# Adding a carried state to the first element of each scan on ScalarE, with VectorE's scans starting from zero

## The chip, the core and the metric

The kernel runs on one core of one Trainium2 chip. The metric is the device time of one execution, in microseconds (us). The core's engines run side by side and meet through semaphores: TensorE (PE; its weight loads are PEld), VectorE (DVE), ScalarE (ACT), GpSimd (POOL) and SyncE (SP), which here issues the DMAs.

## The reference, cut to what matters

The whole reference is a two-layer model: patches and a Fourier embedding, a gated recurrent attention, a mixture of experts, a Mamba block, and a feed-forward part on the upper half of the tokens. Only the Mamba block's recurrence is touched:

```
A = -jnp.exp(A_log)
def step(h, t):
    dt_t, B_t, C_t, u_t = t
    h = h * jnp.exp(dt_t[:, :, None] * A) + (dt_t * u_t)[:, :, None] * B_t[:, None, :]
    y = jnp.einsum('bds,bs->bd', h, C_t)
    return (h, y)
```

There are 4 sequences, 128 inner channels and 32 states for each, so 4096 independent recurrences for each sequence. The value that a recurrence carries is `h`; the factor `exp(dt * A)` is called the decay and the addend `dt * u * B` the input.

## The kernel before, in words

Time is cut into three thirds of G = 368 tokens (index k = 0, 1, 2). One third of one sequence is a segment; the 12 segments run in the order of all four sequences of the first third, then the second, then the third. A segment has NSTEP = 16 steps, one after the other, 192 in all, numbered t. A step handles two halves h = 0 and 1, each 128 recurrences (4 channels by 32 states, on the 128 partitions) over 368 tokens. The recurrence over the tokens of one half is one VectorE instruction, a scan (L1618), `state = decay * state + input`, with an initial state.

What a step t takes, engine by engine:

- PE `spread_input(t)` (L721, two matmuls) spreads the rows of dt*u over the partitions into PSUM banks 2 and 3, and `spread_step(t)` (L731, two matmuls) the rows of dt into banks 4 and 5 or 6 and 7, by the parity of t. `spread_step(t)` waits until both scans of step t-2 are done, because they read the same banks. After it, in even steps, `add_y` (L749, eight matmuls for two steps) sums up the outputs of steps t-4 and t-3; this stands ahead of the next step's matmuls in PE's queue.
- ACT `decay(t)`: two Exp instructions in place in PSUM (all of ACT's calls go through a helper and show as L896), one for each half. Then `carry_on(t-1)` copies the last column of step t-1's two halves into `scan_carry`, for the same rows of the same sequence 64 steps later.
- DVE `input_term(t)` (L1602) multiplies both halves of the spread input by B into the ring buffer `bx`, and `scan_half(t, h)` (L1618) does a scan into `hbuf`.
- POOL `output_term(t)` (L1258) multiplies both halves of `hbuf` by C.

Every fourth step (t % 4 == 3, `shared(t)`) the product with B is POOL's (L1266) and not VectorE's. For that, ACT copies the spread input out of PSUM with `move_input(t+4)`, one cycle of four steps ahead; this copy stands in ACT's queue directly ahead of `decay(t)` of a shared step, and on PE `spread_input(t+4)` stands directly ahead of `spread_step(t)`. The order on VectorE in a cycle around a shared step s is thus: scan(s-2, 1), scan(s-1, 0), scan(s-1, 1), scan(s, 0), input(s+1), scan(s, 1), scan(s+1, 0), input(s+2), scan(s+1, 1), scan(s+2, 0), input(s+3), and so on: four scans in a row around each shared step. The order on each engine is that of the code; nothing rearranges it. Once in a segment VectorE also multiplies the finished outputs by the gate (L1624), and POOL splits the next segment's rows (L1279, L1285).

In the first third (64 steps) a scan starts from the constant 0.0; in the other two (128 steps, 256 scans) its initial state is a column of `scan_carry`.

Of the kernel before, what the change touches and what calls it, by code (L numbers as in the profile page):

```python
# [10 lines left out]
ALU = mybir.AluOpType  # L11
ACT = mybir.ActivationFunctionType
# [3 lines left out]
B, C, T, V = 4, 64, 128, 64  # L16
# [18 lines left out]
DI, DS, DTR, KC = 128, 32, 16, 4  # L35
NSEG = B * NG
NRING = 4
DB = 32
NQ = DB // (128 // DS)
NSTEP = DI // (128 // DS) // 2  # L40
# [36 lines left out]
def build(nc, x, txt, wdft, wts, wexp, bn, out, dbg=None):  # L77
    lay, nw = places(WEIGHTS)
    elay, ne = places(EXPERTS)
    with ExitStack() as ctx:  # L80
# [5 lines left out]
        def s(name):  # L86

            if name not in sems:
                sems[name] = ctx.enter_context(nc.semaphore(name))
            return sems[name]  # L90

        PS = ctx.enter_context(nc.psum_tensor("PS", [128, 8, 512], F32))
# [105 lines left out]
        def shared(t):  # L198
            return t % 4 == 3
# [4 lines left out]
        def own_to(t):  # L204
            return t + 1 - (t + 1) // 4
# [21 lines left out]
        hbuf, hcbuf, bx = ring(0), ring(1), ring(2)  # L227
        carry = sb("scan_carry", [128, B * DS])
# [663 lines left out]
        def _(act):  # L892
# [223 lines left out]
            def decay(t):  # L1116

                seg, i = t // NSTEP, t % NSTEP
                act.wait_ge(s("dt_spread"), t + 1)
                for h in range(2):  # L1120
                    g = (2 * (i % 2) + h) * NQ + i // 2
                    bank = 4 + 2 * (t % 2) + h
                    f(PS[:, bank, 0:G], PS[:, bank, 0:G], ACT.Exp, scale=aneg[:, g:g + 1]).then_inc(s("decay"), 1)

            act.wait_ge(s("a_ready"), 1)
            def move_input(t):

                act.wait_ge(s("x_spread"), inputs_to(t))
                if t >= 4:
                    act.wait_ge(s("bx_ready"), t // 4)  # L1130
                f(moved, PS[:, 2:4, 0:G], ACT.Copy).then_inc(s("x_moved"), 1)

            def carry_on(t):
# [2 lines left out]
                act.wait_ge(s("scanned"), 2 * (t + 1))  # L1136
                f(carry[:, b * DS + 2 * i:b * DS + 2 * i + 2], hbuf[t % NRING][:, :, G - 1], ACT.Copy).then_inc(s("carried"), 1)

            move_input(3)
            for t in range(NSEG * NSTEP):  # L1140
                if shared(t) and t + 4 < NSEG * NSTEP:
                    move_input(t + 4)
                decay(t)
                if 1 <= t <= CARRIED:
                    carry_on(t - 1)
            for g in range(NGR + 2):
                if g < NGR:
                    p, k = groups[g]
                    act.wait_ge(s("mo_ps"), g + 1)
                    f(P1[:, p, cols(k)], PS[:, g % 2, 0:G], ACT.Copy).then_inc(s("mo_ev"), 1)  # L1150
                if g >= 2:
                    p, k = groups[g - 2]
# [25 lines left out]
            for b in range(B):  # L1178
                for y in range(2 * NG):
# [3 lines left out]
                      bias=col("b1a" if y < NG else "b1b")).then_inc(s("hid_ready"), 1)  # L1183
# [125 lines left out]
        def _(dve):  # L1309
# [204 lines left out]
            for n in range(NG * E + 1):  # L1514
# [7 lines left out]
                if n and n % E == 0:  # L1522
                    k = n // E - 1
# [80 lines left out]
            def scan_half(t, h):  # L1604

                seg, i = t // NSTEP, t % NSTEP
                b, k = seg % B, seg // B
                if h == 0:
                    if shared(t):
                        dve.wait_ge(s("bx_ready"), t // 4 + 1)  # L1610
                    else:
                        dve.wait_ge(s("b_used"), own_to(t))
                    if t >= NRING:
                        dve.wait_ge(s("hc_ready"), t - NRING + 1)
                        dve.wait_ge(s("carried"), min(t - NRING + 1, CARRIED))
                dve.wait_ge(s("decay"), 2 * t + h + 1)
                a = b * DS + 2 * i + h
                nc.vector.tensor_tensor_scan(hbuf[t % NRING][:, h, :], PS[:, 4 + 2 * (t % 2) + h, 0:G], bx[t % NRING][:, h, :],  # L1618
                                             carry[:, a:a + 1] if k else 0.0, ALU.mult, ALU.add).then_inc(s("scanned"), 1)

            def finish_y(seg):

# [16 lines left out]
            for g in range(NGR + 2):  # L1639
                if 1 <= g <= NGR:  # L1640
                    p, k = groups[g - 1]
# [6 lines left out]
                if g >= 2:  # L1648
                    p, k = groups[g - 2]
# [154 lines left out]
```

## Time and profile before

| | us |
|---|---|
| median of 3 runs | 1072.88 (1071.45 to 1074.3) |
| the profiled execution's own time | 1069.42 |
| its span, first to last instruction | 1067.3 |
| PE / DVE / ACT / POOL busy | 835.7 / 800.2 / 512.5 / 542.3 |
| the 64 steps with initial state 0.0 | about 489 to 641 of the span |
| the 128 steps with a carried state | about 641 to 955 of the span |

Busy time is an average over stages with different limits; the change acts only in the last line's stage. A row of the timeline gives the start of a group of like instructions, how long the group lasts, and their count; where a bracket stands, the engine had been idle for so long and the named one released it. DVE instructions overlap a little: the next starts before the one ahead has ended.

### The profile page before, as it was taken

Reading aid. Unit: us, or ns where it says so; the run is one execution under the profiler, and the core shown is the slowest. Engines: PE = TensorE matmul, PEld = TensorE weight load, DVE = VectorE, ACT = ScalarE, POOL = GpSimd, SP = SyncE. Lnnn points to the kernel's source line nnn. Section 1 sums busy time; section 2 is a strip of 40 time slices with the busy share of each in tenths; the row PEclk is TensorE's granted clock in tenths of the full one; section 3 lists DMA queues with packets and bytes.
Section 4 is the critical chain, followed back from the end, with each engine's and each line's share of the span. In section 5 each row is a group of like instructions: output and inputs, shape, how many; then the busy total and the mean of one; then the engine's idle time right before and its main releaser. Section 6 shows DMA issues by size and latency. Waiting matters only on the chain.

```text
span 1067.3 us, 11533 instructions
## 1 busy us (share of the span) xinstructions
PE 835.7 (78%) x3813; PEld 356.5 (33%) x3813; DVE 800.2 (75%) x1054; ACT 512.5 (48%) x1015; POOL 542.3 (51%) x356
## 2 busy tenths in 40 slices
PE   7873665767865997976887878878888878879887
PEld 4441334646733333431121111111111111115465
DVE  1248998865532444389999999999999999984475
ACT  1365300185252775664555555555554444434621
POOL 0010749420010000016999999999999999880100
PEclk9987855687565999995667685665556576659987
DMA  9100000700100000011011011011011011000001
GB/s 389 41 0 1 0 0 20 154 1 1 60 1 0 2 2 0 1 29 35 22 43 27 17 43 38 8 40 40 9 38 43 10 34 43 1 0 1 1 16 28
DMA packets 20505, 33.09 MB, mean 31 GB/s; under 512 B 10078, under 2 KB 19294, under 8 KB 19422
## 3 DMA queue, kind: packets, MB, share of 16 engines
q1 hardware_dynamic: 20446, 32.36, 10.7%
q8 instruction: 30, 0.49, 0.2%
q14 instruction: 29, 0.24, 0.1%
HBM read 17.57 MB, written 1.20 MB: 18 GB/s over the span
## 4 chain that ended last, share of the span: by engine, by line
PE 40%; DVE 32%; issue 12%; ACT 9%; POOL 4%; SPq 1%; DMA 1%; DVEq 0%; ACTq 0%; POOLq 0%
DVE pair_arrays L1618 14%; DVE pair_arrays L1602 5%; PE PS L574 4%; PE PS L749 4%; PE PS L721 3%; PE PS L420 3%; PE PS L731 3%; PE PS L510 2%; PE PS L841 2%; ACT PS L896 2%; ACT token_weights L896 2%; PE PS L481 2%; DVE pair_arrays L1424 2%; PE PS L867 2%; ACT pair_arrays L896 2%
## 5 line engine op out<-in xcount | busy, mean ns | idle before, releaser
L1258 POOL TENSOR_TENSOR pair_arrays<-pair_arrays 128x736 f32<-128x736 f32 x192 | 332.4, 1743 | 25.7 <-DVE pair_arrays L1618 25.1
L896 ACT ACTIVATE PS<-PS,A_negative 128x368 f32<-128x368 f32 x384 | 191.3, 538 | 130.1 <-PE PS L731 129.5
L1618 DVE TENSOR_TENSOR_SCAN pair_arrays<-PS,scan_carry,pair_arrays 128x368 f32<-128x368 f32 x256 | 237.1, 972 | 0.4
L1602 DVE TENSOR_TENSOR pair_arrays<-pair_arrays,PS 128x736 f32<-128x736 f32 x144 | 129.7, 901 | 8.4 <-PE PS L721 8.3
L749 PE MATMUL PS<-pair_arrays,weights 128*32 128x368 f32 x768 | 134.1, 730 | 1.2 <-POOL pair_arrays L1258 1.1
L1212 POOL TENSOR_TENSOR big<-pair_arrays 128x1104 f32<-128x1104 f32 (+15 forms) x32 | 55.9, 1766 | 131.1 <-DVE pair_arrays L1375 68.5
L1618 DVE TENSOR_TENSOR_SCAN pair_arrays<-PS,pair_arrays 128x368 f32<-128x368 f32 x128 | 110.6, 909 | 2.7 <-ACT PS L896 2.7
L721 PE MATMUL PS<-spread_rows,token_weights 96*128 96x368 bf16 x192 | 68.5, 452 | 37.8 <-DVE pair_arrays L1602 24.1
L1266 POOL TENSOR_TENSOR pair_arrays<-pair_arrays,token_weights 128x736 f32<-128x736 f32 x48 | 83.9, 1747 | 18.4 <-DVE big L1580 18.4
L721 PE MATMUL PS<-pair_arrays,token_weights 96*128 96x368 bf16 x192 | 67.2, 445 | 25.9 <-DVE pair_arrays L1602 20.1
L481 PE MATMUL PS<-big,weights 128*128 128x368 f32 (+15 forms) x192 | 62.7, 493 | 31.3 <-DVE big L1435 20.1
L1279 POOL TENSOR_TENSOR pair_arrays<-big 128x368 f32<-128x368 f32 x24 | 18.8, 803 | 123.2 <-PE PS L651 123.2
L731 PE MATMUL PS<-pair_arrays,token_weights 96*128 96x368 bf16 x192 | 68.3, 451 | 13.9 <-DVE pair_arrays L1618 12.5
L731 PE MATMUL PS<-spread_rows,token_weights 96*128 96x368 bf16 x192 | 69.9, 460 | 11.0 <-DVE pair_arrays L1618 9.4
L896 ACT ACTIVATE pair_arrays<-pair_arrays 128x69 f32<-128x69 f32 (+4 forms) x46 | 27.7, 607 | 96.3 <-DVE pair_arrays L1424 74.5
L896 ACT ACTIVATE pair_arrays<-PS,weights 128x368 f32<-128x368 f32 (+1 forms) x66 | 38.4, 594 | 53.2 <-PE PS L841 33.0
L481 PEld LDWEIGHTS PS<-big,weights 128*128 128x128 f32 x192 | 45.2, 286 | 49.1 <-issue 30.3
L896 ACT ACTIVATE scan_carry<-pair_arrays 128x2 f32<-128x2 f32 x128 | 26.3, 206 | 69.9 <-DVE pair_arrays L1618 69.5
L896 ACT ACTIVATE token_weights<-PS 128x736 f32<-128x736 f32 (+2 forms) x66 | 44.2, 671 | 29.3 <-PE PS L721 23.9
L574 PE MATMUL PS<-pair_arrays,big 64*64 64x368 f32 x576 | 53.6, 496 | 4.3 <-issue 1.7
L896 ACT ACTIVATE pair_arrays<-PS,bn_shift,bn_scale 128x736 f32<-128x736 f32 x48 | 43.9, 960 | 24.9 <-PE PS L574 24.9
L896 ACT ACTIVATE pair_arrays<-PS 64x256 f32<-64x256 f32 (+5 forms) x48 | 19.8, 426 | 69.4 <-PE PS L510 18.2
(190 smaller groups left out, 1244.1 us busy)
## 6 DMA issues: line engine op xcount, KB each, us to landing
big<-in_x SPq DMA_DIRECT2D x4, 2048.0 KB, 17.3
big<-decay_rows SPq DMA_DIRECT2D x4, 1104.0 KB, 16.3
spread_rows<-pair_arrays SPq DMA_DIRECT2D x96, 46.0 KB, 1.9
pair_arrays<-pair_arrays SPq DMA_DIRECT2D x96, 46.0 KB, 1.9
spread_rows<-big SPq DMA_DIRECT2D x48, 46.0 KB, 1.9
pair_arrays<-big SPq DMA_DIRECT2D x48, 46.0 KB, 1.9
weights<-in_wts SPq DMA_DIRECT2D x1, 2204.0 KB, 18.0
big<-in_wexp SPq DMA_DIRECT2D x1, 1536.0 KB, 7.8
```

Source lines behind the costliest of these rows:

```text
L420: last = nc.tensor.matmul(PS[:, TOK_BANKS[b][i], 0:nm * V], Wtok[:, q].rearrange("p h o -> p (h o)"), xs[:, b, m0:m0 + nm, q, :], start=(q ...
L481: last = nc.tensor.matmul(PS[:, NG * p + k, 0:size], w("ones"), prod[n % 4][:, k * size:(k + 1) * size], start=True, stop=True)
L574: last = nc.tensor.matmul(PS[half((b2 + p) % 2), bank + p, 0:G], weight[half(b2), 64 * b2:64 * b2 + 64], data[half(b2), p, :], start=start ...
L721: last = nc.tensor.matmul(PS[:, 2 + h, 0:G], pick[:, (i // 2) * 128:(i // 2 + 1) * 128], high(stack[seg % 2][1][0:3 * DB, 2 * (i % 2) + h] ...
L731: last = nc.tensor.matmul(PS[:, 4 + 2 * (t % 2) + h, 0:G], pick[:, (i // 2) * 128:(i // 2 + 1) * 128], high(stack[seg % 2][0][0:3 * DB, 2 ...
L749: last = nc.tensor.matmul(PS[r:r + DB, seg % 2, 0:G], w("ysel")[:, (i // 2) * DB:(i // 2 + 1) * DB], hcbuf[t % NRING][:, h, :], start=Fals ...
L896: return nc.scalar.activation(o, i, fn, **kw)
L1212: nc.gpsimd.tensor_tensor(prod[n % 4][:, 0:NC * (L - lag)].rearrange("p (c r) -> p c r", r=L - lag), chunks(q_[:, p, :])[:, :, lag:L], chu ...
L1258: nc.gpsimd.tensor_tensor(hcbuf[t % NRING], hbuf[t % NRING], c4(seg).unsqueeze(1).to_broadcast([128, 2, G]), ALU.mult).then_inc(s("hc_read ...
L1266: nc.gpsimd.tensor_tensor(bx[t % NRING], b4(t // NSTEP).unsqueeze(1).to_broadcast([128, 2, G]), moved, ALU.mult).then_inc(s("bx_ready"), 1)
L1602: tt(bx[t % NRING], b4(seg).unsqueeze(1).to_broadcast([128, 2, G]), PS[:, 2:4, 0:G], ALU.mult).then_inc(s("b_used"), 1)
L1618: nc.vector.tensor_tensor_scan(hbuf[t % NRING][:, h, :], PS[:, 4 + 2 * (t % 2) + h, 0:G], bx[t % NRING][:, h, :], carry[:, a:a + 1] if k e ...
```

## The change

For steps of the second and third third, ScalarE gets two more instructions after `decay(t)`: `bx[:, h, 0] = decay[:, h, 0] * carry + bx[:, h, 0]`, each on one column, with the carry as the scale and the old first input as the bias, both columns in memory with one value for each partition. The scans then all take the constant 0.0 as their initial state, and those with k > 0 wait for the new instruction too.

```diff
+            def carry_in(t):
+
+                b, i = t // NSTEP % B, t % NSTEP
+                act.wait_ge(s("carried"), t - B * NSTEP + 1)
+                act.wait_ge(s("decay"), 2 * t + 2)
+                if shared(t):
+                    act.wait_ge(s("bx_ready"), t // 4 + 1)
+                else:
+                    act.wait_ge(s("b_used"), own_to(t))
+                for h in range(2):
+                    first = bx[t % NRING][:, h, 0:1]
+                    f(first, PS[:, 4 + 2 * (t % 2) + h, 0:1], ACT.Identity, bias=first,
+                      scale=carry[:, b * DS + 2 * i + h:b * DS + 2 * i + h + 1]).then_inc(s("carry_in"), 1)
...
                 decay(t)
+                if t >= B * NSTEP:
+                    carry_in(t)
                 if 1 <= t <= CARRIED:
                     carry_on(t - 1)
...
+                if k:
+                    dve.wait_ge(s("carry_in"), 2 * (t - B * NSTEP) + h + 1)
                 dve.wait_ge(s("decay"), 2 * t + h + 1)
-                a = b * DS + 2 * i + h
                 nc.vector.tensor_tensor_scan(hbuf[t % NRING][:, h, :], PS[:, 4 + 2 * (t % 2) + h, 0:G], bx[t % NRING][:, h, :],
-                                             carry[:, a:a + 1] if k else 0.0, ALU.mult, ALU.add).then_inc(s("scanned"), 1)
+                                             0.0, ALU.mult, ALU.add).then_inc(s("scanned"), 1)
```

ScalarE's queue around a shared step of a carried segment, before: the step ahead, the copy `move_input` (token_weights is the name of its target's memory), the two decays, `carry_on`.

```order
L896 ACTIVATE PS<-PS,A_negative 128x368 [waits dt_spread]
L896 ACTIVATE PS<-PS,A_negative 128x368
L896 ACTIVATE scan_carry<-pair_arrays 128x2 [waits scanned]
L896 ACTIVATE token_weights<-PS 128x736 [waits bx_ready,x_spread]
L896 ACTIVATE PS<-PS,A_negative 128x368 [waits dt_spread]
L896 ACTIVATE PS<-PS,A_negative 128x368
L896 ACTIVATE scan_carry<-pair_arrays 128x2 [waits scanned]
```

The same place of the changed kernel (the memory of `bx` goes by the name pair_arrays):

```order
L896 ACTIVATE PS<-PS,A_negative 128x368 [waits dt_spread]
L896 ACTIVATE PS<-PS,A_negative 128x368
L896 ACTIVATE pair_arrays<-PS,pair_arrays,scan_carry 128x1 [waits b_used,decay,carried]
L896 ACTIVATE pair_arrays<-PS,pair_arrays,scan_carry 128x1
L896 ACTIVATE scan_carry<-pair_arrays 128x2 [waits scanned]
L896 ACTIVATE token_weights<-PS 128x736 [waits bx_ready,x_spread]
L896 ACTIVATE PS<-PS,A_negative 128x368 [waits dt_spread]
L896 ACTIVATE PS<-PS,A_negative 128x368
L896 ACTIVATE pair_arrays<-PS,pair_arrays,scan_carry 128x1 [waits bx_ready,decay,carried]
L896 ACTIVATE pair_arrays<-PS,pair_arrays,scan_carry 128x1
L896 ACTIVATE scan_carry<-pair_arrays 128x2 [waits scanned]
```

The two new instructions stand between the decays and `carry_on` in each of the 128 steps, and the first waits for both decays; no table load was added. On VectorE nothing changes its place. There, before, the two scans of a shared step with the next input between them:

```order
L1618 SCALAR_TENSOR_TENSOR pair_arrays<-PS,scan_carry,pair_arrays 128x368 [waits carried,decay,hc_ready,bx_ready]
L1602 TENSOR_TENSOR pair_arrays<-pair_arrays,PS 128x736 [waits x_spread]
L1618 SCALAR_TENSOR_TENSOR pair_arrays<-PS,scan_carry,pair_arrays 128x368 [waits decay]
```

And in the changed kernel, where L1635 is the scan and L1618 the input:

```order
L1635 SCALAR_TENSOR_TENSOR pair_arrays<-PS,pair_arrays 128x368 [waits carry_in,carried,decay,hc_ready,bx_ready]
L1618 TENSOR_TENSOR pair_arrays<-pair_arrays,PS 128x736 [waits x_spread]
L1635 SCALAR_TENSOR_TENSOR pair_arrays<-PS,pair_arrays 128x368 [waits decay,carry_in]
```

Each scan no longer reads `scan_carry` and has one wait more.

## Rows read from the trace of the kernel before

**Rows 1.** Windows, the carried stage: us, busy of each engine (count), granted clock

```profile
641.00:955.00 314.00, 259.96 (x1036) 57.24 (x1034) 309.42 (x360) 160.58 (x351) 295.62 (x189) 0.61 0.10 26
```

**Rows 2.** The page's costliest groups: count | busy, mean ns of one | idle before

```profile
L896 ACT ACTIVATE PS<-PS,A_negative 128x368 f32<-128x368 f32 x384 | 191.3, 538 | 130.1 <-PE PS L731 129.5
L1618 DVE TENSOR_TENSOR_SCAN pair_arrays<-PS,scan_carry,pair_arrays 128x368 f32<-128x368 f32 x256 | 237.1, 972 | 0.4
L1602 DVE TENSOR_TENSOR pair_arrays<-pair_arrays,PS 128x736 f32<-128x736 f32 x144 | 129.7, 901 | 8.4 <-PE PS L721 8.3
...
L1618 DVE TENSOR_TENSOR_SCAN pair_arrays<-PS,pair_arrays 128x368 f32<-128x368 f32 x128 | 110.6, 909 | 2.7 <-ACT PS L896 2.7
```

**Rows 3.** Timeline of DVE, a carried cycle: start, us, what

```profile
782.48 1.86 DVE L1618 TENSOR_TENSOR_SCAN pair_arrays<-PS,scan_carry,pair_arrays 128x368 f32<-128x368 f32 x2
784.24 0.90 DVE L1602 TENSOR_TENSOR pair_arrays<-pair_arrays,PS 128x736 f32<-128x736 f32 x1
785.05 3.74 DVE L1618 TENSOR_TENSOR_SCAN pair_arrays<-PS,scan_carry,pair_arrays 128x368 f32<-128x368 f32 x4
788.71 0.90 DVE L1602 TENSOR_TENSOR pair_arrays<-pair_arrays,PS 128x736 f32<-128x736 f32 x1
...
794.68 3.73 DVE L1618 TENSOR_TENSOR_SCAN pair_arrays<-PS,scan_carry,pair_arrays 128x368 f32<-128x368 f32 x4
```

**Rows 4.** Timeline of PE in the same cycle

```profile
783.52 0.79 PE L731 MATMUL PS<-pair_arrays,token_weights 96*128 96x368 bf16 x2
784.24 1.46 PE L749 MATMUL PS<-pair_arrays,weights 128*32 128x368 f32 x8
785.63 0.80 PE L721 MATMUL PS<-pair_arrays,token_weights 96*128 96x368 bf16 x2
786.22 0.81 PE L731 MATMUL PS<-pair_arrays,token_weights 96*128 96x368 bf16 x2
```

**Rows 5.** Timeline of ACT in the same cycle

```profile
786.46 0.78 ACT L896 ACTIVATE token_weights<-PS 128x736 f32<-128x736 f32 x1 [0.18 <-PE PS L721]
787.14 0.99 ACT L896 ACTIVATE PS<-PS,A_negative 128x368 f32<-128x368 f32 x2
```

**Rows 6.** Timeline of DVE, a cycle of the first third

```profile
549.09 1.73 DVE L1618 TENSOR_TENSOR_SCAN pair_arrays<-PS,pair_arrays 128x368 f32<-128x368 f32 x2
...
551.55 2.55 DVE L1618 TENSOR_TENSOR_SCAN pair_arrays<-PS,pair_arrays 128x368 f32<-128x368 f32 x3
554.35 0.92 DVE L1618 TENSOR_TENSOR_SCAN pair_arrays<-PS,pair_arrays 128x368 f32<-128x368 f32 x1 [0.26 <-ACT PS L896]
...
563.74 0.92 DVE L1618 TENSOR_TENSOR_SCAN pair_arrays<-PS,pair_arrays 128x368 f32<-128x368 f32 x1 [0.26 <-ACT PS L896]
```

**Rows 7.** Groups of ACT by shape, from none to two column operands

```profile
L896 ACT ACTIVATE pair_arrays<-PS,bn_shift,bn_scale 128x736 f32<-128x736 f32 x48 | 43.9, 960 | 24.9 <-PE PS L574 24.9
L896 ACT ACTIVATE token_weights<-PS 128x736 f32<-128x736 f32 x48 | 37.4, 779 | 25.2 <-PE PS L721 23.9 <-POOL pair_arrays L1266 1.1
...
L896 ACT ACTIVATE router_cols<-PS 77x1 f32<-77x1 f32 x4 | 0.6, 157 | 0.0
```

**Rows 8.** Timeline of ACT, one instruction that waits for ACT's own last

```profile
444.95 1.43 ACT L896 ACTIVATE pair_arrays<-pair_arrays 128x1472 f32<-128x1472 f32 x1
446.42 1.52 ACT L896 ACTIVATE pair_arrays<-pair_arrays,constants 128x1472 f32<-128x1472 f32 x1
```

**Rows 9.** Timeline of DVE at the start of a carried segment

```profile
764.99 3.73 DVE L1618 TENSOR_TENSOR_SCAN pair_arrays<-PS,scan_carry,pair_arrays 128x368 f32<-128x368 f32 x4
...
771.70 0.92 DVE L1602 TENSOR_TENSOR pair_arrays<-pair_arrays,PS 128x736 f32<-128x736 f32 x1 [0.40 <-PE PS L721]
...
776.44 2.73 DVE L1618 TENSOR_TENSOR_SCAN pair_arrays<-PS,scan_carry,pair_arrays 128x368 f32<-128x368 f32 x3
```

**Rows 10.** Timeline of ACT where PE has 2.4 GHz

```profile
776.13 0.20 ACT L896 ACTIVATE scan_carry<-pair_arrays 128x2 f32<-128x2 f32 x1 [1.02 <-DVE pair_arrays L1618]
...
776.91 0.99 ACT L896 ACTIVATE PS<-PS,A_negative 128x368 f32<-128x368 f32 x2
```

## The prediction

> **What bounds the kernel now.** I read the page first, to find the stage that the change touches, then the windows. In the carried stage VectorE is busy for 309.42 of 314 us [rows 1]. That looks like a plain VectorE bound, and by it anything that shortens a scan is a gain. The page's groups [rows 2] give the hope a size: a scan whose initial state is a column takes 972 ns, one that starts from the constant 909, so 63 ns, 256 times: 16.1 us. But the idle time after the scans from zero names ACT, and that sent me to the timeline, to see how long VectorE would stay busy if it were faster.
>
> One cycle of four steps around a shared step s [rows 3]: the two scans at 782.48 are scan(s-3, 1) and scan(s-2, 0); input(s-1) follows at 784.24; the four from 785.05 are scan(s-2, 1), scan(s-1, 0), scan(s-1, 1), scan(s, 0). The next four begin at 794.68, a period of 9.63. VectorE alone would need eight scans and three inputs. A pair of scans goes by at 784.24 - 782.48 = 1.76, and an input at 785.05 - 784.24 = 0.81, so 4 x 1.76 + 3 x 0.81 = 9.47. The missing 0.1 to 0.15 is in the group of four: it ends at 788.79, so its last scan starts at 788.79 - 0.97 = 787.82, where three pitches of 0.88 would have put it at 787.70. What it waited for is in [rows 5]: decay(s) starts at 787.14, and its first half ends 0.54 later [rows 2], at 787.68. The scan starts 0.13 behind that.
>
> So there is a second chain, and it is as long as VectorE's own work. It starts at E, the end of scan(s-3, 1), 782.48 + 0.97 = 783.45:
> - PE: spread_step(s-1) at 783.52, add_y at 784.24, spread_input(s+4) at 785.63, ended 786.43 [rows 4];
> - ACT: move_input at 786.46, decay(s) at 787.14, its first half ended 787.68 [rows 5];
> - DVE: scan(s, 0) at 787.82.
>
> From E to that scan, 4.36. The first third confirms that this chain decides as soon as scans are shorter [rows 6]: scan(s-3, 1) starts at 549.09 and ends at 550.00; scan(s, 0) starts at 554.35, again 4.35 later, but now with 0.26 of idle time ahead of it that ACT ended. The period there is 563.74 - 554.35 = 9.39. Eight scans shorter by 63 ns should have saved 0.50 of 9.63, and saved 0.24: the rest is wait.
>
> **The change, part by part.** (a) *The scans* lose 63 ns each. From scan(s, 0) to the next E, VectorE works without a wait: in the first third 9.39 - 4.35 = 5.04, in the carried stage 9.63 - 4.36 = 5.27. With scans from zero I take 5.04.
>
> (b) *The wait.* scan(s, 0) waited for the first decay alone; now it waits for both decays and then for a new ACT instruction. Terms on the chain from E:
> - the second decay: the pair takes 0.99 and the first 0.54 [rows 2, 5], so 0.45;
> - ACT's wait for its own decay: 446.42 - (444.95 + 1.43) = 0.04 [rows 8]. Three semaphores are waited for, so it may cost another 0.05; I take 0.04, and 0.09 as the upper end;
> - the new instruction itself. No row shows one column with a scale and a bias column. The copy of one column takes 157 ns without operands, and over 736 columns two column operands turn 779 into 960 [rows 7], so 181 for both: 157 + 181 = 338 ns, 0.34. The lower end is the bare 0.16, the upper 0.40.
>
> The last hop from ACT to VectorE was 0.13 and stays. Sum: 0.45 + 0.04 + 0.34 = 0.83, with ends 0.60 and 0.94. The chain becomes 4.35 + 0.83 = 5.18 (4.95 to 5.29).
>
> The Trainium skill, page "ScalarE: Activation LUTs", section "What ACT_TABLE_LOAD costs", says that each [128,1] pointer operand adds about 93 ns to a base of 186 ns. The trace agrees on the operand (181 for two); by the page alone the instruction would be 186 + 2 x 93 + 1 = 373 ns, and the chain 0.03 longer. An estimate from that page only, which makes the case slightly worse for the change.
>
> (c) *The new period* is 5.18 + 5.04 = 10.22, against 9.63: +0.59 for each ordinary cycle at PE's lower clock.
>
> (d) *The other steps.* An own step's new instruction must also wait for its input term on VectorE. input(s+1) starts 0.82 behind scan(s, 0) (the pitch of scans from zero: (2.55 - 0.91) / 2 [rows 6]) and lasts 0.90, then 0.05, 0.34 and 0.13: ready 2.24 behind it; VectorE reaches scan(s+1, 0) at 0.82 + 0.81 + 0.82 = 2.45. Hidden, by 0.2. For scan(s+2, 0) and scan(s+3, 0) the window from the end of the scan two steps back is 2 x 0.82 + 0.81 - 0.09 = 2.36; spread_step, both decays and the new instruction need 0.07 + 0.76 + 0.04 + 1.00 + 0.04 + 0.34 + 0.13 = 2.38. That is even; a delay there is taken out of the wait at the next shared step, which hangs on E and not on them. ACT has room: 160.58 busy in 314 [rows 1], plus 128 x about 0.6 = 77.
>
> (e) *Segment starts.* Eight of the 32 cycles hold a segment's start. They are longer now: from the last of four scans at 764.99 + 3.73 - 0.97 = 767.75 to the next such scan at 776.44 + 2.73 - 0.97 = 778.20 [rows 9], 10.45. In it are the gate product and 0.40 of waiting for PE, which is itself late because POOL's outputs are. When VectorE stands still for 0.8 in each cycle, POOL and PE have caught up, and the gate product falls into the same wait: these cycles also take 10.22, 0.2 less than now.
>
> (f) *PE's clock.* It is 0.61 on average here [rows 1], so (0.61 - 0.5) / 0.5 = 22% of the time is at 2.4 GHz. There the PE part is short, and ACT waits for VectorE instead [rows 10]: the copy of step s-2 at 776.13 follows the end of scan(s-2, 1), at about 776.10, and decay(s) ends at 777.90. With 0.04 + 0.34 + 0.13, scan(s, 0) could start at 778.41, 2.31 behind that end, where VectorE needs 2 x 0.82 - 0.09 = 1.55. So it waits there too, by 0.76; the period is 8 x 0.82 + 3 x 0.81 + 0.76 = 9.75, 0.47 less than at 1.2 GHz.
>
> Sum: before, 314 us for 128 steps. After, 32 x 10.22 = 327.0, less 7 cycles (22% of 32) x 0.47 = 3.3, gives 323.7. Change +10. Without any time at 2.4 GHz, +13. I take +11: PE will be less busy, and may be granted its upper level less often. The profiled execution took 1069.42 with a span of 1067.3; so 1080.4. The median of the runs is 3.5 above that execution; on it the forecast is 1072.88 + 11 = 1084.
>
> **The rivals.**
> 1. *Hidden on ScalarE, faster.* ACT is half idle and could do the new work in VectorE's shadow. Then each scan's 63 ns comes through: 16 us at most (1057), and with the wait of [rows 6] kept, 32 x 0.24 = 8 (1065). It decides if the chain grows by less than 9.63 - 5.04 - 4.35 = 0.24. Against it: the second decay alone is 0.45. For it: the chain is pieced together from one cycle of each kind, and another cycle may start it elsewhere. 0.09.
> 2. *No change*, the two effects cancelling: it needs a chain that grows by 0.24, give or take 3.2 / 32 = 0.10. 0.07.
> 3. *The scans don't get shorter.* The 63 ns may come from the stage and not from the operand: the row shows only that scans without it are earlier. Then the stretch behind scan(s, 0) stays 5.27, the period is 10.45, and the sum 334.4 - 3.3 - 314 = +17: 1090. Nothing else differs between the stages (same shapes, same memories), so 0.06.
> 4. *More steps stall.* (d) leaves 0.01 to 0.2 on own steps. If the semaphore hops cost 0.1 more each, so 0.2 on the chain and 0.1 on scan(s+1, 0), a cycle is 0.3 longer, another 9.6 us: 1094. 0.13.
>
> My own case, 1077 to 1091, has 0.65.
>
> **How the numbers follow.** The own case's ends: chain terms at 0.60 give 32 x 0.23 = 7 us less (1077), terms at 0.94 and no 2.4 GHz give 3.5 and 3.3 more (1091). The range reaches down to 1076 and up to 1094, leaving out the faster cases and a tail of rival 4. A measurement of this kernel can tell 0.3%, 3.2 us, from no change. Faster 0.09, same 0.07, slower 0.84.
>
> **What would show it.** In the changed trace: scans of the carried stage at about 909 ns; the new instructions at about 0.34; an idle time of some 0.8 to 1.2 us ahead of one scan in every four steps, put down to ACT, some 25 to 35 us in all; none to speak of ahead of other scans; VectorE busy for about 293 of 325. The prediction is wrong if idle time ahead of scans is under 10 us, if the scans stay at 972, or if scan(s+1, 0) and the inputs wait as well.

## The result, and the profile after

| | before | after |
|---|---|---|
| median, us | 1072.16 (1071.25 to 1074.3) | 1092.26 (1089.83 to 1093.98) |
| the profiled execution's time | 1069.42 | 1089.83 |
| its span | 1067.3 | 1087.8 |
| PE / DVE / ACT / POOL busy | 835.7 / 800.2 / 512.5 / 542.3 | 844.9 / 787.0 / 584.1 / 539.4 |

The change made the kernel slower: ratio 1.0183 [1.0156, 1.021], +20 us. The forecast was +11, with 1084 for the median. The measured 1092.26 lies near the upper end of its range of 1076 to 1094, and 1.3 above the 1077 to 1091 that it gave to its own case.

The page's costliest groups of the changed kernel (the first three answer to [rows 2]; L1635 is the scan, L1618 the input, L896 with `scan_carry` among its inputs the new instruction):

```profile
L1635 DVE TENSOR_TENSOR_SCAN pair_arrays<-PS,pair_arrays 128x368 f32<-128x368 f32 x384 | 336.0, 910 | 36.8 <-ACT pair_arrays L896 28.4
...
L896 ACT ACTIVATE PS<-PS,A_negative 128x368 f32<-128x368 f32 x384 | 191.3, 538 | 74.7 <-PE PS L731 74.4
...
L1618 DVE TENSOR_TENSOR pair_arrays<-pair_arrays,PS 128x736 f32<-128x736 f32 x144 | 129.1, 896 | 1.8 <-PE PS L721 1.8
...
L896 ACT ACTIVATE pair_arrays<-PS,pair_arrays,scan_carry 128x1 f32<-128x1 f32 x256 | 76.2, 347 | 36.4 <-DVE pair_arrays L1618 29.3
```

The windows of the carried stage, now 641 to 976; it answers to [rows 1] (there 314 us):

```profile
641.00:976.00 335.00, 277.44 (x1042) 55.53 (x1038) 298.96 (x361) 232.47 (x607) 297.33 (x190) 0.57 0.10 24
```

The same stretch by groups, the scans alone:

```profile
L1635 DVE TENSOR_TENSOR_SCAN pair_arrays<-PS,pair_arrays 128x368 f32<-128x368 f32 x257 | 226.6, 911 | 34.4 <-ACT pair_arrays L896 28.4 <-POOL pair_arrays L1274 2.0 <-ACT scan_carry L896 1.8
```

VectorE's busy time fell from 309.42 to 298.96 us, though the window is 21 us longer. (Summed one by one, the scans take 15 us less. An instruction that stands behind a wait doesn't overlap the one ahead of it, and that takes 4.5 back.) Against this gain stand 34.4 us of idle time ahead of scans, where all of VectorE's idle time in the window of before was 4.6. 28.4 of the 34.4 are put down to the new instruction, and 29.6 lie ahead of scan(s, 0). In this stage no input waits; the 1.8 us of the page's row lie elsewhere.

The timeline of DVE through one cycle of the changed kernel; it answers to [rows 3]:

```profile
789.44 1.93 DVE L1635 TENSOR_TENSOR_SCAN pair_arrays<-PS,pair_arrays 128x368 f32<-128x368 f32 x2
791.29 0.90 DVE L1618 TENSOR_TENSOR pair_arrays<-pair_arrays,PS 128x736 f32<-128x736 f32 x1
792.10 2.54 DVE L1635 TENSOR_TENSOR_SCAN pair_arrays<-PS,pair_arrays 128x368 f32<-128x368 f32 x3
795.70 0.92 DVE L1635 TENSOR_TENSOR_SCAN pair_arrays<-PS,pair_arrays 128x368 f32<-128x368 f32 x1 [1.05 <-ACT pair_arrays L896]
796.54 0.89 DVE L1618 TENSOR_TENSOR pair_arrays<-pair_arrays,PS 128x736 f32<-128x736 f32 x1
...
806.05 0.92 DVE L1635 TENSOR_TENSOR_SCAN pair_arrays<-PS,pair_arrays 128x368 f32<-128x368 f32 x1 [1.04 <-ACT pair_arrays L896]
```

And the chain that feeds the scan at 795.70, on PE (as [rows 4]):

```profile
790.42 0.79 PE L731 MATMUL PS<-pair_arrays,token_weights 96*128 96x368 bf16 x2
791.14 1.46 PE L749 MATMUL PS<-pair_arrays,weights 128*32 128x368 f32 x8
792.53 0.80 PE L721 MATMUL PS<-pair_arrays,token_weights 96*128 96x368 bf16 x2
```

and on ACT (as [rows 5]):

```profile
793.36 0.78 ACT L896 ACTIVATE token_weights<-PS 128x736 f32<-128x736 f32 x1
794.04 0.99 ACT L896 ACTIVATE PS<-PS,A_negative 128x368 f32<-128x368 f32 x2
795.12 0.59 ACT L896 ACTIVATE pair_arrays<-PS,pair_arrays,scan_carry 128x1 f32<-128x1 f32 x2
```

The three scans from 792.10 are scan(s-2, 1), scan(s-1, 0) and scan(s-1, 1); then VectorE stands still for 1.05 until scan(s, 0). It can't start: `move_input(s+4)`, both decays and the new instruction run one behind another, and the new one ends at 795.12 + 0.35 = 795.47. The period is 806.05 - 795.70 = 10.35, against 9.63 in [rows 3]. From E, 789.44 + 0.92 = 790.36, to the scan it is 5.34; from the scan to the next E 5.02.

### The profile page after: what moved, and what is told of

It is laid out like the page before. It is cut to its first block and busy times, and to the rows that moved or that the text cites. A ratio compares the mean times of both kernels' runs of the same rounds, so it can differ in the third digit from the quotient of the medians.

```text
span 1087.8 us, 12045 instructions
## 1 busy us (share of the span) xinstructions
PE 844.9 (78%) x3813; PEld 356.3 (33%) x3813; DVE 787.0 (72%) x1054; ACT 584.1 (54%) x1271; POOL 539.4 (50%) x356
## 5 line engine op out<-in xcount | busy, mean ns | idle before, releaser
L1635 DVE TENSOR_TENSOR_SCAN pair_arrays<-PS,pair_arrays 128x368 f32<-128x368 f32 x384 | 336.0, 910 | 36.8 <-ACT pair_arrays L896 28.4
L896 ACT ACTIVATE PS<-PS,A_negative 128x368 f32<-128x368 f32 x384 | 191.3, 538 | 74.7 <-PE PS L731 74.4
L749 PE MATMUL PS<-pair_arrays,weights 128*32 128x368 f32 x768 | 138.3, 718 | 4.4 <-POOL pair_arrays L1274 4.2
L1618 DVE TENSOR_TENSOR pair_arrays<-pair_arrays,PS 128x736 f32<-128x736 f32 x144 | 129.1, 896 | 1.8 <-PE PS L721 1.8
L721 PE MATMUL PS<-spread_rows,token_weights 96*128 96x368 bf16 x192 | 66.7, 442 | 41.7 <-DVE pair_arrays L1618 27.4
L896 ACT ACTIVATE pair_arrays<-PS,pair_arrays,scan_carry 128x1 f32<-128x1 f32 x256 | 76.2, 347 | 36.4 <-DVE pair_arrays L1618 29.3
L721 PE MATMUL PS<-pair_arrays,token_weights 96*128 96x368 bf16 x192 | 65.9, 437 | 36.4 <-DVE pair_arrays L1618 29.4
L896 ACT ACTIVATE pair_arrays<-pair_arrays 128x69 f32<-128x69 f32 (+4 forms) x46 | 27.6, 607 | 96.2 <-DVE pair_arrays L1440 76.0
L731 PE MATMUL PS<-spread_rows,token_weights 96*128 96x368 bf16 x192 | 68.2, 450 | 9.7 <-DVE pair_arrays L1635 8.7
L731 PE MATMUL PS<-pair_arrays,token_weights 96*128 96x368 bf16 x192 | 67.4, 445 | 9.9 <-DVE pair_arrays L1635 8.8
L896 ACT ACTIVATE pair_arrays<-PS,weights 128x368 f32<-128x368 f32 (+1 forms) x66 | 38.5, 594 | 55.6 <-PE PS L841 34.4
L896 ACT ACTIVATE pair_arrays<-PS 64x256 f32<-64x256 f32 (+5 forms) x48 | 19.8, 426 | 74.8 <-PE PS L420 21.4
L896 ACT ACTIVATE pair_arrays<-PS,bn_shift,bn_scale 128x736 f32<-128x736 f32 x48 | 43.9, 960 | 24.9 <-PE PS L574 24.9
L896 ACT ACTIVATE token_weights<-PS 128x736 f32<-128x736 f32 (+2 forms) x66 | 44.2, 671 | 19.5 <-PE PS L721 13.5
L721 PEld LDWEIGHTS PS<-spread_rows,token_weights 96*128 96x128 bf16 x192 | 12.1, 106 | 119.1 <-DVE pair_arrays L1618 79.5
```

The costliest lines, as they stand in the source:

```text
L721: last = nc.tensor.matmul(PS[:, 2 + h, 0:G], pick[:, (i // 2) * 128:(i // 2 + 1) * 128], high(stack[seg % 2][1][0:3 * DB, 2 * (i % 2) + h] ...
L731: last = nc.tensor.matmul(PS[:, 4 + 2 * (t % 2) + h, 0:G], pick[:, (i // 2) * 128:(i // 2 + 1) * 128], high(stack[seg % 2][0][0:3 * DB, 2 ...
L749: last = nc.tensor.matmul(PS[r:r + DB, seg % 2, 0:G], w("ysel")[:, (i // 2) * DB:(i // 2 + 1) * DB], hcbuf[t % NRING][:, h, :], start=Fals ...
L896: return nc.scalar.activation(o, i, fn, **kw)
L1618: tt(bx[t % NRING], b4(seg).unsqueeze(1).to_broadcast([128, 2, G]), PS[:, 2:4, 0:G], ALU.mult).then_inc(s("b_used"), 1)
```

## The experiments

Theory A, in the expectations, is that of the prediction: the chain from E through PE and ACT to scan(s, 0) sets the period, and what lengthens it is paid once in four steps. The other places where the loss could arise are ScalarE's added work in itself, the own steps (all but the shared ones), and VectorE's waits; the expectations say which number each would give. Ratios are to the kernel before, on the same chip, with their 95% intervals.

A time is that of the whole program, and only the carried stage is in question. The table has both. The middle column is the difference of the medians. The third is how long the stage takes in the profiled execution: from the start of the last scan(s, 0) of the first third to that of the last one of the program, 32 cycles. The last column is the rest of that execution's span.

| | time against before, us | the 32 cycles, us | rest of the span, us |
|---|---|---|---|
| before | | 314.7 | 752.6 |
| the change | +20.1 | 332.9 | 754.8 |
| e1_zero_only | -9.3 | 303.6 | 759.0 |
| e2_act_only | -0.9 | 313.3 | 758.4 |
| e3_interleave | +9.0 | 320.7 | 755.1 |
| e4_own_only | +3.1 | 312.7 | 762.5 |
| e5_shared_only | +22.5 | 334.3 | 758.7 |
| e6_one_wait | +16.3 | 329.3 | 757.1 |
| e7_later_sums_before | +9.1 | 321.4 | 756.4 |
| e7_later_sums_after | +24.6 | 336.5 | 757.3 |
| e8_split_sums_before | +5.1 | 317.5 | 756.3 |
| e9_own_interleaved | -4.5 | 309.5 | 755.8 |
| e10_own_interleaved_split | -3.9 | 318.8 | 754.3 |
| e11_all_interleaved_split | +3.3 | 316.1 | 759.6 |

The rest differs by up to 10 us between executions, also where its program is the same as before (it is changed in e7, e8, e10 and e11 alone, whose sums move in the first third too). So a difference of a few us in the time is no proof of one in the stage.

### e1_zero_only: the scans' gain alone

The kernel before, with every scan from 0.0. The carried state is left out of the computation.

```diff
-                                             carry[:, a:a + 1] if k else 0.0, ALU.mult, ALU.add)
+                                             0.0, ALU.mult, ALU.add)
```

> All scans start from 0.0 and there is no new ScalarE work: the carried state is left out of the computation. Theory A (two chains of equal length: the shortened scans only uncover the wait for PE and ScalarE at each shared step): ordinary cycles fall from 9.62 to 9.39 as in the first third, so 5 to 9 us faster than before, with 0.2 to 0.3 us of idle time ahead of each shared step's first scan. Rival (VectorE alone bounds the stage): 16 us faster.

0.9914 [0.9897, 0.9932], 1063.89 us: 9.3 less. Two cycles of DVE's timeline:

```profile
794.71 0.93 DVE L1617 TENSOR_TENSOR_SCAN pair_arrays<-PS,pair_arrays 128x368 f32<-128x368 f32 x1 [0.26 <-ACT PS L896]
...
804.09 0.92 DVE L1617 TENSOR_TENSOR_SCAN pair_arrays<-PS,pair_arrays 128x368 f32<-128x368 f32 x1 [0.26 <-ACT PS L896]
```

Period 9.38, as in [rows 6] (9.39), and the same 0.26 of waiting at the shared step. Even with the new work at no cost, the time gains 9.3 of the 16 us, and the profiled stage 11.2. Ordinary cycles at PE's lower level pay the old chain's 0.26; where the sums of the chain take 0.83, at the upper level (2.4 GHz), most take 9.02 to 9.05, with no wait at all.

### e2_act_only: ScalarE's instructions alone

The 256 instructions are issued at their places, but write two spare columns that no scan reads; the scans are those of before and wait for none of them. The instruction, against that of the change:

```diff
-                    f(first, PS[:, 4 + 2 * (t % 2) + h, 0:1], ACT.Identity, bias=first,
+                    f(spare[:, h:h + 1], ONE, ACT.Identity, bias=EPS5,
```

> The two new ScalarE instructions with their waits stand where the change puts them, but read and write columns that nobody else uses; the scans are those of before and don't wait for them. Theory A (what costs is the wait of the scan, not ScalarE's time): within 2 us of before. Rival (ScalarE's queue becomes too full, so decays come late at every step): most of the 20 us loss.

0.9995 [0.9985, 1.0004]: nothing. The windows of 641 to 955 show that the work was there:

```profile
641.00:955.00 314.00, 259.57 (x1048) 56.63 (x1040) 310.15 (x362) 240.91 (x609) 296.51 (x189) 0.64 0.11 26
```

ACT is busy for 240.91 us against 160.58 in [rows 1], and the 32 cycles take 313.3 us (314.7 before). Here 80 us of work on a half idle engine cost nothing; it is the wait for it that costs.

### e5_shared_only and e4_own_only: which steps pay

The change in the 32 shared steps alone, and in the 96 own steps alone; the others scan from `scan_carry` as before. The diff is that of e5; in e4 both conditions say `not shared(t)`.

```diff
-                if t >= B * NSTEP:
+                if t >= B * NSTEP and shared(t):
                     carry_in(t)
...
+                folded = k and shared(t)
...
-                                             0.0, ALU.mult, ALU.add)
+                                             0.0 if folded or not k else carry[:, a:a + 1], ALU.mult, ALU.add)
```

> The change in the 32 shared steps alone; the 96 own steps keep scan_carry as initial state. Theory A (the loss is the longer wait at each shared step): cycles of 5.34 + 5.15 = 10.5 us, so 20 to 25 us slower than before, at least as slow as the whole change. Rival (each step pays the same): 1/4 of the loss, 5 us slower.

1.0209 [1.0195, 1.0224], +22.5 us. The page's groups of its scans, from zero and with a column:

```profile
L1637 DVE TENSOR_TENSOR_SCAN pair_arrays<-PS,pair_arrays 128x368 f32<-128x368 f32 x192 | 169.4, 912 | 30.0 <-ACT pair_arrays L896 26.7
L1637 DVE TENSOR_TENSOR_SCAN pair_arrays<-PS,scan_carry,pair_arrays 128x368 f32<-128x368 f32 x192 | 178.0, 965 | 0.0
```

The ordinary period is 10.49, E to scan(s, 0) again 5.34. A quarter of the change makes the whole loss and more (the 32 cycles take 334.3, the change's 332.9): 26.7 us of waiting for the new instruction, and none where a scan has its old form.

> The change in the 96 own steps alone; the 32 shared steps keep scan_carry as initial state and have no new instruction. Theory A (the loss arises at the shared steps alone, waits at own steps are taken out of the wait at the next shared one): 2 to 6 us faster than before. Rival (every step pays the same): 3/4 of the loss, 15 us slower than before.

1.0025 [1.001, 1.004], +3.1 us, where 2 to 6 less were expected: a miss in the time. In the stage it is none: the 32 cycles took 312.7 us in the profiled execution, 2.1 less than before. What that execution lost, it lost in the rest of the program (762.5 against 752.6), where the two kernels are the same: 6.6 us behind the recurrence, at a granted clock of 0.76 against 0.83 before, and 3.3 ahead of it. Why the clock differed, and what the other executions did, the trace doesn't say. The ordinary cycles were as expected (9.52, and 4.35 to scan(s, 0)). More could have been gained, for four of the eight cycles with a segment's start took 11.1, against 10.3 to 10.8 before. DVE's timeline in one of them:

```profile
695.19 0.92 DVE L1618 TENSOR_TENSOR pair_arrays<-pair_arrays,PS 128x736 f32<-128x736 f32 x1 [0.75 <-PE PS L721]
696.02 0.92 DVE L1637 TENSOR_TENSOR_SCAN pair_arrays<-PS,pair_arrays 128x368 f32<-128x368 f32 x1
697.46 0.92 DVE L1637 TENSOR_TENSOR_SCAN pair_arrays<-PS,pair_arrays 128x368 f32<-128x368 f32 x1 [0.52 <-POOL pair_arrays L1274]
```

and ACT's:

```profile
695.80 1.00 ACT L896 ACTIVATE PS<-PS,A_negative 128x368 f32<-128x368 f32 x2 [1.95 <-PE PS L731]
696.88 0.59 ACT L896 ACTIVATE pair_arrays<-PS,pair_arrays,scan_carry 128x1 f32<-128x1 f32 x2
```

PE is late there, since it does the next segment's D product too. The first input waits 0.75 for it, and then the own step's scan waits 0.52 more. The row puts this down to POOL, but the new instruction ends at 696.88 + 0.35 = 697.23, 0.23 ahead of the scan, the same last hop as at 795.70; the first decay ended at 695.80 + 0.54 = 696.34, before VectorE was free. An own step's new instruction is hidden only while PE is ahead.

### e3_interleave: the second decay taken off the chain

The change, with each half's new instruction directly behind that half's decay.

```diff
...
                 for h in range(2):
...
+                    f(PS[:, bank, 0:G], PS[:, bank, 0:G], ACT.Exp, scale=aneg[:, g:g + 1]).then_inc(s("decay"), 1)
...
+                    act.wait_ge(s("decay"), 2 * t + h + 1)
                     first = bx[t % NRING][:, h, 0:1]
-                    f(first, PS[:, 4 + 2 * (t % 2) + h, 0:1], ACT.Identity, bias=first,
+                    f(first, PS[:, bank, 0:1], ACT.Identity, bias=first,
                       scale=carry[:, b * DS + 2 * i + h:b * DS + 2 * i + h + 1]).then_inc(s("carry_in"), 1)
...
```

> The change with another order on ScalarE: decay of half 0, new instruction of half 0, decay of half 1, new instruction of half 1. Theory A (the chain to the shared step's first scan holds the second decay): 0.45 us leaves it, the cycle falls from 10.36 to about 9.9, so some 14 us faster than the change and 4 to 7 us slower than before. Rival (the extra instructions and semaphores cost at every step): as slow as the change, 20 us above before.

1.0081 [1.0061, 1.0102], +9 us, 11 less than the change; the 32 cycles took 320.7 us, 6.0 more than before and 12.2 less than in the change. The ordinary period is 9.94 and E to scan(s, 0) 4.91, which is 5.34 less the 0.43 of the second decay: the term has the size that the prediction gave it. The time is some 2 us above the expected 4 to 7, the stage within it.

### e6_one_wait: the last hop

In the changed kernel the scans of half 0 wait for five semaphores. Two of these waits (the decay, and the input term) are implied by the new instruction's own, and are dropped.

```diff
...
                 if k:
                     dve.wait_ge(s("carry_in"), 2 * (t - B * NSTEP) + h + 1)
-                dve.wait_ge(s("decay"), 2 * t + h + 1)
+                else:
+                    dve.wait_ge(s("decay"), 2 * t + h + 1)
```

> The change, with the waits of the carried scans on decay and on the input taken away, which the new instruction's semaphore already implies. The hop from the new instruction to the scan was 0.23 us, where the hop from decay was 0.13 before. Theory A (each further pair of semaphores on a scan costs its own wait instruction of 0.05 us and its start, behind one another): hop back to 0.13, cycle 10.26, 3 us faster than the change, 17 us slower than before. Rival (the hop is long because of what the new instruction writes): no faster than the change, 20 us slower than before.

1.0152 [1.0137, 1.0166]: 16.3 us above the kernel before (1089.09 against 1072.76), where the change was 20.1 above it. One period of DVE:

```profile
796.15 0.92 DVE L1637 TENSOR_TENSOR_SCAN pair_arrays<-PS,pair_arrays 128x368 f32<-128x368 f32 x1 [1.05 <-ACT pair_arrays L896]
...
806.41 0.92 DVE L1637 TENSOR_TENSOR_SCAN pair_arrays<-PS,pair_arrays 128x368 f32<-128x368 f32 x1 [1.04 <-ACT pair_arrays L896]
```

10.26, 0.10 less than the change's 10.36; the 32 cycles took 329.3 us, 3.6 less. The chain's ACT rows end with the new instruction:

```profile
805.93 0.59 ACT L896 ACTIVATE pair_arrays<-PS,pair_arrays,scan_carry 128x1 f32<-128x1 f32 x2
```

805.93 + 0.35 = 806.28, and the scan follows at 806.41, 0.13 later, where it was 0.23 (795.47 to 795.70). The last hop is 0.13 again when the two waits are gone, in all but one of the 32 cycles. The trace shows why, for the waits are instructions of their own in VectorE's queue, for one or two semaphores each. Those of the scans in the carried stage of the change (ns at the least, in the middle and at the most):

```profile
L1633 DVEq EVENT_SEMAPHORE  x128: 49/50/50, 641.9 to 972.4; - x128
L1634 DVEq EVENT_SEMAPHORE  x256: 21/35/50, 642.0 to 972.7; - x128
```

Ahead of the scan at 795.70 the first, which has the new instruction's semaphore, stands at 795.51, and the second, with the decay's, at 795.61. In e6 there is only one, at 806.32 for the scan at 806.41. Before, the decay's own was the last, at 787.72 for the scan at 787.81, and one that was met earlier stood ahead of it; the hop was 0.13 with four semaphores. So it isn't the number of waits that costs, but a wait instruction that stands behind the one that is met last: 0.10.

### e7_later_sums_before and e7_later_sums_after: PE's part of the chain moved

`add_y` moved to odd steps, out of the chain from E, in the kernel before and in the changed one.

```diff
-                if t % 2 == 0 and t >= 4:
-                    add_y(t - 4)
-                    add_y(t - 3)
+                if t % 2 and t >= 5:
+                    add_y(t - 5)
+                    add_y(t - 4)
```

> The kernel before, with PE's output sums (add_y) moved from the even steps to the odd ones, behind the matmuls of the shared step instead of ahead of them. Theory A (the second chain leads through these sums and is just as long as VectorE's work): ordinary cycles fall from 9.62 to 9.47, 2 to 5 us faster. Rival (they are hidden): no change. If GpSimd then waits for the sums, slower.

> The change, with the same move of PE's output sums. Theory A: the chain then starts at scan(s-2, 1) and is 0.87 + 1.0 + 0.08 + 0.35 + 0.23 = 2.5 us long, so the cycle falls from 10.36 to about 10.0: 8 to 12 us faster than the change, 8 to 12 us slower than before. Rival (PE has no part in the wait, ScalarE alone sets it): as slow as the change.

Both missed: 1.0082 [1.0066, 1.0098] and 1.0234 [1.0213, 1.0255], both slower by 4 to 9 us than without the move. DVE in the first, around a shared step:

```profile
788.02 3.60 DVE L1618 TENSOR_TENSOR_SCAN pair_arrays<-PS,scan_carry,pair_arrays 128x368 f32<-128x368 f32 x4
792.00 0.92 DVE L1602 TENSOR_TENSOR pair_arrays<-pair_arrays,PS 128x736 f32<-128x736 f32 x1 [0.38 <-PE PS L721]
```

The four scans run without a gap; the wait has moved to input(s+1), whose `spread_input` now stands behind the eight matmuls. In both places that were tried, ahead of the shared step's matmuls and behind them, something that VectorE needs next stands behind the 1.4 us of the sums.

### e8_split_sums_before: half the sums at a time

The kernel before, with the sums of one step, not two, ahead of the chain's `spread_input(s+4)`, and the other one's a step later.

```diff
-                if t % 2 == 0 and t >= 4:
-                    add_y(t - 4)
-                    add_y(t - 3)
+                if t >= 4 and t % 4 != 1:
+                    add_y(t - 4)
+                    if t % 4 == 0:
+                        add_y(t - 3)
```

> The kernel before, with PE's sums split: of the two steps summed up ahead of a shared step's matmuls, the second is summed behind them, in the shared step itself. Theory A: 0.7 us leaves the chain to the shared scan, and no other wait takes its place, since the next input has 0.5 us of slack: ordinary cycles 9.47 for 9.62, 2 to 4 us faster. Rival (as with the sums moved whole): PE's full queue hands the wait to the next input, slower.

1.0053 [1.0035, 1.0072], a miss. PE's timeline shows why:

```profile
793.28 1.44 PE L749 MATMUL PS<-pair_arrays,weights 128*32 128x368 f32 x4
...
795.99 1.46 PE L749 MATMUL PS<-pair_arrays,weights 128*32 128x368 f32 x8
```

Four of these matmuls take as long as eight (1.44 against 1.46). In the trace the eight start as two bunches of four, the four of a bunch within 0.02 us of each other. (The code calls four matmuls for two steps, one for each group of 32 columns; the trace has two records of each, and the two of a column group run one behind the other.) Splitting them makes two stays on PE of one, and input(s+1) waits for the second.

### e9_own_interleaved, e10 and e11: a version that gains

e9 puts together what held: own steps only, interleaved, without the implied waits; shared steps keep `scan_carry`. e10 is e9 with the sums split as in e8. e11 is e10 with the shared steps changed too. `both(t)` is the interleaved form of e3. From the diff of e9 against the kernel before:

```diff
...
-                decay(t)
+                if t >= B * NSTEP and not shared(t):
+                    both(t)
+                else:
+                    decay(t)
...
```

> The new instruction in own steps alone, each half's directly behind its decay, and without the implied waits on VectorE; shared steps keep scan_carry. Ordinary cycles stay at 9.52 as with own steps alone. Theory A (there the segment starts lost 0.5 us, since the late decays of that place got the second decay and the new instruction on top): segment starts back to about 10.6, 1 to 3 us faster than before. Rival (own steps cost by themselves): 3 us slower, as with own steps alone.

0.9964 [0.9952, 0.9975], 1068.22 us, faster than both kernels; the 32 cycles took 309.5 us, 5.2 less than before. DVE around a shared step:

```profile
784.93 2.54 DVE L1645 TENSOR_TENSOR_SCAN pair_arrays<-PS,pair_arrays 128x368 f32<-128x368 f32 x3
787.67 0.98 DVE L1645 TENSOR_TENSOR_SCAN pair_arrays<-PS,scan_carry,pair_arrays 128x368 f32<-128x368 f32 x1 [0.19 <-ACT PS L896]
```

The shared scan waits 0.19, for its decay alone, and most ordinary cycles take 9.2 to 9.5. Cycles with a segment's start take 9.9 to 10.6, where e4 had up to 11.11. What the interleaving and the dropped waits each do for it wasn't parted.

> Both together: own steps interleaved, shared steps on scan_carry, PE's sums split. Theory A: neither chain binds, VectorE works through 9.02 + 0.13 = 9.15 us in an ordinary cycle: 24 x 9.15 + 8 x 10.5 = 304 for 314, 8 to 12 us faster than before. If another wait (GpSimd's or PE's queue) is next, 0 to 5 us faster.

> As the one before, but the shared steps too start from zero and wait for the new instruction. Theory A: the shared scan then hangs on scan(s-2, 1): 0.87 + 0.54 + 0.08 + 0.35 + 0.13 = 1.97 us behind it where VectorE needs 1.55, a wait of 0.4 and a cycle of 9.4 to 9.5: 3 to 6 us faster than before, and slower than with shared steps on scan_carry. If the wait at the shared step were harmless: at least as fast as that one.

0.9982 [0.9959, 1.0005] and 1.0028 [1.0014, 1.0041], both above their expectations. e10 has cycles of 9.33 to 9.36, but also of 10.0 to 10.1, where input(s+1) waits for PE as in e8; its profiled execution, at 1075.25, is one of its longer ones (the median is 1068.81). The medians of e11 and e10 are 7 us apart (1076.02 for e11), as theory A wants of a kernel that puts the new instruction ahead of scan(s, 0). The traces show the wait, 0.58 ahead of scan(s, 0) in e11's cycles of 9.70 against 0.12 in e10's of 9.33 (0.4 and 9.4 to 9.5 were expected), but not the sum: the 32 cycles took 316.1 us in e11 and 318.8 in e10. So for this pair theory A isn't shown.

## Why the prediction was right, and where it was short

**In short.** The direction and the mechanism were right; the loss was nearly twice the +11. The time fell into the range only because its upper end had been stretched to 1094 for rival 4, of which a part came true; in so far it was luck.

**The bound and the second chain: right.** E to scan(s, 0) was 4.36 in [rows 3] and is 5.34 after. e5 and e4 place the loss in the shared steps, e2 excludes ScalarE's time, and e3 and e6 take 0.43 and 0.10 off the period by taking them off the chain.

**(a) The scans: right.** 910 ns, and 5.02 from the scan to the next E (forecast 5.04). Rival 3 is out.

**(b) The chain: the mechanism was right, two terms were too small.** Forecast 5.18, measured 5.34. The new instruction takes 347 ns (forecast 0.34; the estimate of 373 beside it was too high), the second decay is worth 0.43 (0.45). ACT's wait for its own decay is 795.12 - (794.04 + 0.99) = 0.09, at the upper end that was given, where 0.04 was taken. And "the last hop from ACT to VectorE was 0.13 and stays" was wrong: it is 0.23, and e6 shows that the two implied waits are what costs 0.10, by the wait instruction behind the new instruction's. Together 0.15 in each of 32 cycles, nearly 5 us. This is the smaller half of rival 4 (hops dearer by 0.1), which put all of it at 1094; its other half, a stall at scan(s+1, 0), isn't in the timeline. The lower end of the terms was added up wrongly: 0.45 + 0.04 + 0.16 is 0.65, not 0.60; nothing hangs on it.

**(c) The period.** 10.36 against the forecast 10.22. With the ordinary 9.62 of before that is +0.74 a cycle.

**(d) The own steps: right in ordinary cycles.** scan(s+1, 0) doesn't wait. The pair at 789.44, scan(s-3, 1) and scan(s-2, 0), lasts 1.93 where two scans without a wait last 1.73 (the pair at 797.35), so the second waits for 0.2; it stands behind E, and the delay is taken out of the wait at the shared step, as forecast. In sum 4.8 of the 34.4 us stand ahead of own steps' scans, where "none to speak of" was forecast. e4 shows the limit of "hidden": at segment starts, with PE late, it costs some 0.5.

**(e) Segment starts: about right.** They do fall into the same wait, but take 10.1 to 10.7 rather than 10.22. The 32 cycles are 332.9; 32 x 10.36 would be 331.5. Of the 1.4 between them the starts add 0.8. The rest is in four other cycles: those that end at 712.85, 775.21 and 889.30 are 0.2 to 0.35 longer, the last one 0.14 shorter. What holds the three up wasn't looked into.

**(f) PE's clock: the step that failed.** Seven cycles at 2.4 GHz were to take 9.75, which is 0.47 less, 3.3 us in all. Neither the count nor the price came true. The granted clock is 0.57 in the stage, but the sums of the chain take under 1.3 us, less than the 1.46 of the lower level, in only three of the 32 cycles, against nine before. These three are all segment starts; they take 10.34, 10.12 and 10.60, and in the first and the last of them scan(s-2, 0) waits 0.27 and 0.44 for its own new instruction. Elsewhere the upper level misses the chain. PE's timeline shows one stretch of it that ends too early:

```profile
862.24 0.50 PE L721 MATMUL PS<-pair_arrays,token_weights 96*128 96x368 bf16 x2 [1.13 <-DVE pair_arrays L1618]
...
863.07 0.80 PE L731 MATMUL PS<-pair_arrays,token_weights 96*128 96x368 bf16 x2 [0.34 <-DVE pair_arrays L1635]
863.80 1.46 PE L749 MATMUL PS<-pair_arrays,weights 128*32 128x368 f32 x8
```

The pair at 862.24 takes 0.50, PE at its upper level; the chain's own part, from 863.07, takes 0.80 and 1.46, at the lower. PE had waited for VectorE between the groups of the stretch before. Whether the longer waits themselves move these stretches off the chain wasn't tried.

The price was wrong too. The changed kernel has no ordinary cycle with fast sums, but e6 has two, of 10.10 and 10.13 against its 10.27: 0.15 less, not 0.47. PE in the first:

```profile
874.08 0.83 PE L749 MATMUL PS<-pair_arrays,weights 128*32 128x368 f32 x8
875.44 0.79 PE L721 MATMUL PS<-pair_arrays,token_weights 96*128 96x368 bf16 x2 [0.53 <-DVE pair_arrays L1618]
```

The sums are done at 874.91, but `spread_input(s+4)` waits 0.53 more for VectorE's input(s-1), which reads the same banks. The prediction had left this wait out: it took the cycle at the upper level from [rows 10], a segment's start, and let `carry_on(s-2)` on ACT wait for scan(s-2, 1) instead. So even seven such cycles would have given back 1 us.

**The sum.** For these 32 cycles the forecast was 323.7, and 332.9 were measured. The 9.2 are 32 x (10.36 - 10.22) = 4.5 of (b), the 1.4 that (e) tells of, and the 3.3 of (f). The stage grew by 332.9 - 314.7 = 18.2 and the span by 20.5; the other 2.3 lie behind the recurrence, where the program is the same. From 40 to 60 us behind the last scan the granted clock was 1.00 in the trace of before and 0.86 in that of after. One execution of each doesn't say whether the change brings that about, and the table has larger differences in the rest of the span.

**What would show it.** Scans at 909: 910. New instruction 0.34: 0.347. One scan in four idle for 0.8 to 1.2: 1.05. Idle in all 25 to 35: 34.4, of which 30.2 put down to ACT. VectorE busy 293 of 325: 299 of 335, since a scan behind a wait doesn't overlap the one ahead of it.

**The other rivals.** Rival 1 (faster) is refuted in its mechanism: the work is free (e2), but not where it delays scan(s, 0). Its upper case, 16 us, was never to be had (e1: 9.3, and 11.2 in the stage). Rival 2 needed 0.24 more on the chain, and 0.98 came.

## What to carry to other kernels

An engine busy for 98% of a stage may have a second chain just as long beside it; follow back what released the last instruction ahead of which it idles, in a stage where it is a little faster, before you price a saving on it. Work moved to a half idle engine is free until something that is on such a chain waits for it: put it only on the steps whose scans have slack, as e9 does, and behind the half that needs it, not behind both. Look at each wait of the instruction that ends the chain: drop those that another implies. A share of time at a clock level is no share of cycles to be credited: look in the rows whether it falls on the chain, and which wait is next when the chain gets shorter. And read the stage beside the time: here the rest of the program varied by as much as half of the effect.

## What the runs showed of the hardware

- A scan of 128x368 float32 takes 972 ns with a column as its initial state and 910 with a constant. The price goes with the operand and not with the step: 965 and 912 side by side in e5, 976 and 908 in e4, where the two kinds of step have changed places.
- A wait that is already met isn't free if it stands in an instruction behind the one that is met last: the scan started 0.23 behind the new instruction with one such wait instruction in between, 0.13 without it (the change and e6). One that stood ahead of it cost nothing (before: 0.13 too).
- Of the eight records of matmuls with 32 output columns, four start within 0.02 us, and the next four about 0.6 behind them; so four that go to only two of the column groups took 1.44 us, as long as eight (e8). The Trainium skill, page "TensorEngine Tiling (Array Packing)", section "Key Properties", says that different tiles of the array can load and multiply in parallel; the trace agrees.
- One column through ScalarE with a scale column and a bias column takes 347 ns (379 in e2, where all its operands are in SBUF); two in a row take 0.59.
